# Two 16x16-head cross attentions: from folded context queries with turned probabilities to projected keys and values on 32-row and 32-column tiles

## The reference, cut to what matters

```python
qh = (q @ Wq + bq).reshape(B, LQ, HEADS, D_K).transpose(0, 2, 1, 3)      # LQ 64, HEADS 16, D_K 16
kh = (k @ Wk + bk).reshape(B, LKV, HEADS, D_K).transpose(0, 2, 1, 3)     # LKV 1601
vh = (v @ Wv + bv).reshape(B, LKV, HEADS, D_K).transpose(0, 2, 1, 3)
scores = jnp.einsum('bhqd,bhkd->bhqk', qh, kh) * scale                   # scale 1/4
attn = jax.nn.softmax(scores, axis=-1)
out = jnp.einsum('bhqk,bhkd->bhqd', attn, vh)
return concat @ Wo + bo
```

## Time and profile before

| what | value |
|---|---|
| three runs | 6370.2, 6377.44, 6382.16 us |
| the profiled execution, span from first to last instruction | 6363.3 us |
| its own time apart from the span | none is listed; the median lies 14.1 us above the span |
| TensorE busy, mean granted clock | 5521.9 us (87%), 0.901 |
| VectorE, ScalarE, GpSimd busy | 3835.9, 2546.1, 1134.8 us |

### The profile page before, as it was taken

How to read it: one execution, slowest core, us unless ns; L and a number is a source line. 1 busy time by engine, 2 the same in 40 slices (tenths; PEclk the granted TensorE clock), 3 DMA queues, 4 the chain that set the end, 5 groups by cost and what they waited for, 6 DMA issues and landing times. The chain is left out here.

```text
span 6363.3 us, 96853 instructions
## 1 busy us (share of the span) xinstructions
PE 5521.9 (87%) x33712; PEld 4579.4 (72%) x33712; DVE 3835.9 (60%) x7029; ACT 2546.1 (40%) x5011; POOL 1134.8 (18%) x545
## 2 busy tenths in 40 slices
PE   6789999976898999998655999885699899999877
PEld 4578888954797988886212888771499798889465
DVE  5367777725444767775797443457533677777453
ACT  1145555511444555553221333340244455555121
POOL 0022222100121001110363212234222111010200
PEclk8899999996899999999766999997799999999985
DMA  1010000001110000000111111123110100000020
GB/s 57 26 32 14 19 20 14 7 34 47 40 46 27 19 20 13 19 19 18 40 46 40 47 52 40 48 67 93 50 49 26 28 18 19 19 19 6 28 88 27
DMA packets 224813, 213.50 MB, mean 34 GB/s; under 512 B 54595, under 2 KB 201892, under 8 KB 216260
## 3 DMA queue, kind: packets, MB, share of 16 engines
q1 hardware_dynamic: 220356, 200.15, 10.3%
q10 hardware_dynamic: 4096, 8.40, 0.5%
HBM read 170.61 MB, written 2.23 MB: 27 GB/s over the span
## 5 line engine op out<-in xcount | busy, mean ns | idle before, releaser
L844 PE MATMUL PS<-context_turned,queries 128*128 128x512 f32 x4800 | 1127.3, 379 | 70.6 <-issue 54.2
L905 ACT CAST probs_turned<-PS 128x512 fp32r<-128x512 f32 x1600 | 726.6, 510 | 904.5 <-PE PS L856 904.5
L876 PE MATMUL PS<-probs_turned,context_part 128*128 128x256 f32 (+2 forms) x8112 | 1069.2, 286 | 8.1 <-DVE weighted L953 8.1
L919 DVE TENSOR_TENSOR probs_turned<-PS,probs_turned 128x512 fp32r<-128x512 f32 x1600 | 866.1, 583 | 299.8 <-ACT probs_turned L905 293.7
L844 PEld LDWEIGHTS PS<-context_turned,queries 128*128 128x128 f32 x4800 | 853.6, 194 | 235.7 <-issue 64.5
L876 PEld LDWEIGHTS PS<-probs_turned,context_part 128*128 128x128 f32 (+1 forms) x8112 | 996.0, 189 | 9.1 <-DVE probs_turned L919 9.1
L911 ACT ACTIVATE probs<-PS,minus_max 128x1024 f32<-128x1024 f32 (+1 forms) x800 | 747.6, 936 | 197.8 <-DVE minus_max L964 195.4
L959 DVE TENSOR_REDUCE row_max<-PS 128x1 f32<-128x1024 f32 (+1 forms) x800 | 757.1, 981 | 104.8 <-PE PS L844 104.1
L856 PE MATMUL PS<-ident,probs 128*128 128x128 f32 (+1 forms) x5200 | 734.5, 278 | 16.7 <-DVE probs_turned L919 13.1
L856 PEld LDWEIGHTS PS<-ident,probs 128*128 128x128 f32 (+1 forms) x5200 | 577.3, 140 | 62.9 <-issue 18.3
L1632 PE MATMUL PS<-input_part,part_up 128*128 128x512 f32 x2304 | 552.6, 392 | 18.5 <-DVEq L1713 8.6
(11 more groups left out here) (373 smaller groups left out, 6483.9 us busy)
## 6 DMA issues: line engine op xcount, KB each, us to landing
context_rows<-in_ctx SPq DMA_DIRECT2D x56, 768.0 KB
raw_up<-in_L_ffn_W SPq DMA_DIRECT2D x16, 1024.0 KB, 4.8
raw_down<-in_L_ffn_W SPq DMA_DIRECT2D x16, 1024.0 KB, 4.8
b_all<-bc_turned SPq DMA_DIRECT2D x16, 512.0 KB, 3.6
c_all<-bc_turned SPq DMA_DIRECT2D x16, 512.0 KB, 4.7
raw_up<-in_L_ffn_wg_w SPq DMA_DIRECT2D x8, 1024.0 KB, 4.8
raw_down<-in_L_ffn_w_w SPq DMA_DIRECT2D x8, 1024.0 KB, 4.8
raw_second<-in_L_ffn_w_w SPq DMA_DIRECT2D x8, 1024.0 KB, 6.9
```

The costliest lines, as they stand in the source:

```text
L844: last = nc.tensor.matmul(S[:, 512 * j:512 * j + cols], qs[a][:, v, p * P:(p + 1) * P], yT[b][:, v, 512 * j:512 * j + cols], start=(m == 0 ...
L876: last = nc.tensor.matmul(O_ps, yp[a][0:kk, u, k, :], probsT[b][0:kk, par, k, :], start=(k == 0 and m == 0), stop=(k == KT - 1 and m == 2))
L905: nc.scalar.copy(out, bank).then_inc(t_act.sem, 1)
L919: nc.vector.tensor_tensor(rest, bank, lead, ALU.subtract).then_inc(t_dve.sem, 1)
```

## The change

Both sublayers get an attention of their own, `head_attention`; `small_xattn` is rewritten around it. 16 dimensions of Wq are loaded per head instead of 32 (the DMA picks 16 of every 32 columns), so the queries need two chunks of 128 rows instead of four. `masked_queries` writes each chunk twice, with every other head zeroed: ScalarE writes the even heads and VectorE, after it, the odd ones, so that the 32 rows of two heads by 128 columns are one operand for both heads. Keys (turned, 256 x 1601) and values (1601 x 256, with a column of ones behind each head for the row sum) are made per batch with float32 matmuls. Scores are made twice in float32: as rows (128 queries x 512 keys), from which only the maximum is taken, and turned (128 keys x 128 queries, with the maximum subtracted by a matmul with ones into the same bank), from which ScalarE makes the exponentials that are the moving operand of the weighted sum as they are. No probability is transposed. Score matmuls use 32 rows of the array each, for four pairs of heads i = 0 to 3 into four banks; the weighted sum uses 128 rows and 17 columns at 32-column offsets, also four at a time, into one bank.

A batch is 7 units (`turns`) of two key tiles or one block of 512 keys, the last one short. A cycle t does the turned scores of unit t, values of unit t+10, the weighted sum of unit t-1, keys of unit t+12, row scores of unit t+8, and in L1 the context transposes of unit t+13 (four of the seven units); in L3 the context, stored turned to DRAM by L1, is loaded turned. There are 112 units and 13 + 3 further cycles around them. Two score fills per cycle share a ring of six banks; everything else (values, the turned maximum, the spread row sums, keys, context) shares one bank, `side`, and the weighted sum has the eighth. Every loop is written out, no hardware loop is left in these sublayers. Wo is loaded into four chunks of 128 rows of which half are zero, so `linear_rows` runs over 4 chunks instead of 2, and `turn_sums` goes.

```diff
@@ -1877,37 +1877,555 @@
 def l1_xattn(core):
-    small_xattn(core, "L1_xattn_", True)
+    small_xattn(core, "L1_xattn_", True, True)
...
-def small_xattn(core, pre, biased):
-
-    heads, d, pad = 16, 16, 32
-    X = core.X
+    small_xattn(core, "L3_xattn_", False, False)
+
+
+def small_xattn(core, pre, biased, first):
...
+        w = weights(core, own, pre, WkT=[P, 4, CDIM], Wv=[P, DIM])
+        w["Wq"] = core.sb(own, "wq", [P, DC, DIM])
+        loads = w.loads + [(w["Wq"][:, c, :].rearrange("p (h d) -> p h d", d=16),
+                            core.dram[pre + "Wq"][:, c, :].rearrange("p (h e) -> p h e", e=32)[:, :, 0:16], landed)
+                           for c in range(DC)]
...
-        sums = core.sb(own, "sums", [P, BATCH, heads // 2, d])
-        qT = core.sb(own, "qT", [P, heads * pad // P, TOKENS])
-        room = ContextRoom(core, own, 1, heads * pad // P, P // pad)
...
+        room = TurnedContext(core, own, first)
+        Q = core.sb(own, "queries", [P, DC, BATCH, 2 * SEQ])
+        oT = core.sb(own, "oT", [P, 4, TOKENS])
+        wo = core.sb(own, "wo_grouped", [P, 4, DIM])
+        made = HeadConstants(core, own, biased)
         with ExitStack() as front:
             U = core.sb(front, "u", [P, TILES, DIM])
             uT = core.sb(front, "uT", [P, DC, TOKENS])
-            normalize(core, X, U, loads=w.loads + room.loads, clear=room.q_tile, turned=(uT, None, None))
-            linear_turned(core, uT, w["Wq"], qT, w["bq"] if biased else None)
-        wv4 = w["Wv"][:].rearrange("c (a p d) -> c p a d", a=2, d=d)
-        context_attention(core, room, qT, head_queries(w["WkT"]), 4, heads * SEQ, False, None,
-                          lambda pair: wv4[:, pair], sums, heads // 2, 2, 2, 2, d ** -0.5, d)
-        oT = core.sb(own, "oT", [P, DC, TOKENS])
-        turn_sums(core, sums, heads // 2, d, oT, w["bv"])
-        linear_rows(core, oT, w["Wo"], X, w["bo"] if biased else None, X)
+            with nc.allow_non_contiguous_dma(reason="two bias rows of 256 numbers"):
+                normalize(core, X, U, loads=loads + room.loads, turned=(uT, None, None))
+            masked_queries(core, uT, w, Q, made, biased)
+        head_attention(core, room, Q, made, w["Wv"], biased, wo, core.dram[pre + "Wo"], oT, 0.25)
+        linear_rows(core, oT, wo, X, w["bo"] if biased else None, X)
...
+def masked_queries(core, src, w, Q, made, biased):
...
+            for f in range(fills):
+                m, half = f // HALVES, f % HALVES
+                for c in range(DC):
+                    last = nc.tensor.matmul(PS[:, f, :], w["Wq"][:, c, m * P:(m + 1) * P], src[:, c, half * 512:(half + 1) * 512],
+                                            start=(c == 0), stop=(c == DC - 1))
+                last.then_inc(ready.sem, 1)
...
+                nc.scalar.activation(out, bank, ACT.Identity, bias=made.bq[:, c, 0:1] if biased else 0.0,
+                                     scale=mask[:, 0:1]).then_inc(by_act.sem, 1)
...
+class TurnedContext:
...
+        self.y = [core.sb(own, "context_turned", [CDIM, KEYS]) for _ in range(2)]
+        self.landed = core.semaphores("context_landed", 2)
+        if first:
+            self.rows = [core.sb(own, "context_rows", [P, KT, CDIM]) for _ in range(2)]
...
+def head_attention(core, room, Q, made, wv, biased, wo, wo_rows, oT, scale):
...
+    s_lead, v_lead, k_lead, c_lead = 8, 10, 12, 13
+    ring, banks, side, out_bank = 3, 6, 6, 7
...
+    turn_at, spread_at = -1, 8
...
+    def st_fill(t):
+        return 4 * (min(t + s_lead, total) + t)
+
+    def s_fill(t):
+
+        return 4 * ((t + s_lead) + min(max(t + 1, 0), total))
+
+    def wait_fill(pe, fill):
+
+        if fill < banks:
+            return
+        old = fill - banks
+        for t in cycles:
+            if unit(t) is not None and st_fill(t) <= old < st_fill(t) + 4:
+                pe.wait_ge(exp_done.sem, exp_done.at(t * 4 + old - st_fill(t) + 1))
+            if unit(t + s_lead) is not None and s_fill(t) <= old < s_fill(t) + 4:
+                pe.wait_ge(max_done.sem, max_done.at((t + s_lead) * 4 + old - s_fill(t) + 1))
...
+        kT = core.sb(own, "keys_turned", [P, 2, DC, KEYS])
+        V = core.sb(own, "values", [P, 2, KT, heads, wide])
+        probs = core.sb(own, "probs_turned", [P, ring, groups, 2, DC, P])
+        part = core.sb(own, "block_max", [P, 2, DC, groups, 4])
+        M = core.sb(own, "row_max", [P, groups, 32])
+        shift = core.sb(own, "minus_max", [P, 2, DC, P], F32R)
+        ones = core.sb(own, "ones_wide", [P, P], F32R)
+        O = core.sb(own, "weighted", [P, 2, 4 * SEQ])
...
+                        sp.wait_ge(side_dve.sem, side_dve.at(dve_no["context", b * turns + context_fills - 1] + 1))
+                        sp.dma_start(core.dram["ctx_turned"][b], room.y[b % 2][:]).then_inc(stored[b % 2].sem, 16)
...
+                def wait_side(fill):
+                    n = fill_no[fill]
+                    if n:
+                        by, count = taken_by[n - 1]
+                        pe.wait_ge(by.sem, by.at(count + 1))
...
+                    for k in range(4 * j, min(4 * j + 4, KT)):
+                        kk = keys_of[k]
+                        last = nc.tensor.transpose(PS[:, side, (k - 4 * j) * P:(k - 4 * j) * P + kk], room.rows[b % 2][0:kk, k, :],
+                                                   core.ident[0:kk, 0:kk])
+                    last.then_inc(side_ready.sem, 1)
...
+                    for n, c in enumerate(chunks):
+                        last = nc.tensor.matmul(PS[:, side, n * cols:(n + 1) * cols], wk[:, c * P:(c + 1) * P],
+                                                room.y[b % 2][:, lo:lo + cols], start=True, stop=True)
+                    last.then_inc(side_ready.sem, 1)
...
+                    for n, kt in enumerate(tiles_of(j)):
+                        kk = keys_of[kt]
+                        last = nc.tensor.matmul(PS[0:kk, side, n * DIM:(n + 1) * DIM], room.y[b % 2][:, kt * P:kt * P + kk], wv[:],
+                                                start=True, stop=True)
+                    last.then_inc(side_ready.sem, 1)
...
+                    for i in range(groups):
+                        wait_fill(pe, s_fill(t) + i)
+                    for n, c in enumerate(chunks):
+                        for i in range(groups):
+                            rows = slice(32 * i, 32 * i + 32)
+                            last = nc.tensor.matmul(PS[:, (s_fill(t) + i) % banks, n * cols:(n + 1) * cols], Q[rows, c, b, :],
+                                                    kT[rows, b % 2, c, lo:lo + cols], start=True, stop=True)
+                    last.then_inc(s_ready.sem, 1)
...
+                    for i in range(groups):
+                        wait_fill(pe, st_fill(t) + i)
+                    many = len(tiles_of(j))
+                    for i in range(groups):
+                        rows = slice(32 * i, 32 * i + 32)
+                        nc.tensor.matmul(PS[:, (st_fill(t) + i) % banks, 0:many * 2 * P].rearrange("p (k s) -> p k s", k=many), ones[rows, :],
+                                         shift[rows, b % 2].rearrange("p c s -> p (c s)").unsqueeze(1).broadcast_to([32, many, 2 * P]),
+                                         start=True, stop=False, skip_group_check=True)
+                    for n, kt in enumerate(tiles_of(j)):
+                        kk = keys_of[kt]
+                        for c in range(DC):
+                            at = (n * DC + c) * P
+                            for i in range(groups):
+                                rows = slice(32 * i, 32 * i + 32)
+                                last = nc.tensor.matmul(PS[0:kk, (st_fill(t) + i) % banks, at:at + P],
+                                                        kT[rows, b % 2, c, kt * P:kt * P + kk], Q[rows, c, b, :],
+                                                        start=False, stop=True, skip_group_check=True)
+                    last.then_inc(st_ready.sem, 1)
...
+                    for n, kt in enumerate(tiles_of(j)):
+                        kk = keys_of[kt]
+                        for c in range(DC):
+                            for a in range(2):
+                                g = 2 * c + a
+                                for i in range(groups):
+                                    last = nc.tensor.matmul(PS[32 * i:32 * i + wide, out_bank, g * SEQ:(g + 1) * SEQ],
+                                                            V[0:kk, b % 2, kt, 8 * a + 4 * c + i, :],
+                                                            probs[0:kk, t % ring, i, n, c, a * SEQ:(a + 1) * SEQ],
+                                                            start=(kt == 0 and g == 0), stop=(kt == KT - 1), skip_group_check=True)
+                    last.then_inc(av_done.sem, 1)
...
+                for t in cycles:
+                    if unit(t) is not None:
+                        scores_turned(t)
```

(46 more changed lines are left out.)

310 lines of the change are left out of this document (305 added, 5 removed).

## The result

Five runs of the changed kernel have a median of 6321.36 us (6317.11 to 6333.05), five of the kernel before 6377.44 us (6349.16 to 6389.2). The ratio is 0.9924, with an interval of 0.9906 to 0.9943: 56 us less, where 263 were forecast. The direction was right, the size was not, and 6321 lies just outside the range, which ended at 6310.

What follows compares the result with a forecast made beforehand. TensorE was taken to bound the kernel, busy for 87% of 6363.3 us. Attention blocks -154 and -116 us, ends +7, total -263, gave a span of 6100 and a median of 6114 us; range for 8 in 10: 5900 to 6310.

Steps and rivals of the forecast that it cites:

- the prices of the records: TensorE in both attention blocks: float32 records cost 0.43 us for 512 columns, 0.22 for 256, 0.11 for 128.
- full overlap of the tiles: Scores and weighted sum: four float32 tiles run in about the time of one, 0.055 us a round of 64 columns.
- the changes of shape: Each attention cycle: four changes of tile shape at 0.2 us each, 28 a batch, 5.6 us.
- TensorE waits for the maxima once a cycle: Before the turned scores: 1.5 us in six cycles, 0.7 in the short one, 9.7 us a batch.
- B: Turned scores, row scores, weighted sum: tiles overlap by about three quarters, 30% more, +182 us, 6296 in all; chance 0.18.
- D: Weighted sum: column tiles reading the same 128 rows take turns, 22.8 instead of 5.7 us, +547, 6661; chance 0.06.
- Rival A: Both attention blocks: loads slip under the drain, so the 5.6 us of shape changes vanish, -179 us, 5935; chance 0.15.
- a batch at full clock, L3 and L1: Attention blocks: work, shape changes and waits sum to 47.7 us a batch in L3, 50.3 in L1.
- filling and emptying: Pipeline's 13 cycles of filling and 3 of emptying: +10 us in each block, bounds 0 and 40.
- fronts and ends: Around both attention blocks: front at zero (bounds -5 and +15), end +3.6 us for more Wo records less `turn_sums`.
- twice a batch a fill of the shared bank follows directly on another: Turned maximum after values, keys after spread sums: TensorE waits 0.9 us each, 1.8 us a batch.
- Rival C: Both attention blocks: TensorE's idle time drops the clock, at 1.2 GHz +1160 us, 7270 in all; chance 0.09.

Runs made afterwards that it cites:

- the copy: Against the changed kernel, the spread row sums are copied out of the shared bank first and inverted from SBUF: 6243.07 us, ratio 0.9799 to the kernel before.
- the busy wait: Against the changed kernel, ten records of an unread identity product run on TensorE while it waits for the division: 6264.43 us, ratio 0.9824 to the kernel before.
- the kernel of all together: Changed kernel plus copy before division, values first, busy filling, ScalarE's context copy and a later wait for GpSimd's constants: 5986.9 us, 0.9389 to the kernel before.
- one moved call: Against the changed kernel, values are made before the turned scores in cycles without context transposes just before: 6111.03 us, ratio 0.9604 to the kernel before.

## Why the prediction was wrong in size

**Right: the prices of the records, full overlap of the tiles, the changes of shape, and that TensorE waits for the maxima once a cycle.** Rivals B and D fall: 64 weighted records of 17 columns and 128 rows take 1.02 us from start to start, change of shape included, where 16 x 0.055 + 0.2 = 1.08 was priced and D had four times the records' part. The 8 row-score records on four row tiles take 1.14 us and the 2 key records on the full array 1.13, so four tiles cost what one costs, to 0.01 us. The Trainium skill, in "TensorE: Matmul & The Clock Gate", Measured speedup vs the span model, gives 3.07 for four row tiles; the measurement here decides, and it says 4. Rival A falls too: priced at 0.86 to 0.88 us, the bursts are 1.02 to 1.06 us apart, so that 0.14 to 0.20 us for the change of shape are in every one. The Trainium skill's rule in "TensorEngine Tiling (Array Packing)", Key Properties, that a change of mode drains the engine, agrees with it.

**Wrong: three terms (the waits of a batch, no loss of clock in the steady cycles, the filling), and a rival that was taken as all or nothing.** Between the two profiled executions -263 was forecast and 6326.3 - 6363.3 = -37 measured, 226 us apart. They go to these steps:

| step of the prediction | forecast | measured | part of the 226 us |
|---|---|---|---|
| a batch at full clock, L3 and L1 | 47.7, 50.3 | 50.6, 52.0 | 16 x 2.9 + 16 x 1.7 = 74 |
| the clock in the steady cycles | no loss | 54.3 - 50.6, 53.5 - 52.0 | 16 x 3.7 + 16 x 1.5 = 83 |
| filling and emptying | +10 each | block less 16 middle batches: 26 in L3, 46 in L1 | 52 |
| fronts and ends | +3.6 each | +5.7 in L3, +11.1 in L1 | 10 |
| the unchanged code, mostly from L1's end to L3's start | 0 | 1969.9 after, 1963.6 before | 7 |

The first row holds the step "twice a batch a fill of the shared bank follows directly on another, 0.9 us each". It took every evacuation of that bank for a copy of 0.69 us. One of them is a reciprocal of 256 columns, and that takes 1.76 us:

```profile
L2383 DVE RECIPROCAL row_scale<-PS 128x256 f32<-128x256 f32 x16 | 28.1, 1758 | 34.6 <-PE PS L2284 34.6
```

This could have been read before. The kernel before has reciprocals of other widths (VectorE by shape, the kernel before):

```profile
L552 DVE RECIPROCAL row_sum<-row_sum 128x16 f32<-128x16 f32 x24 | 6.1, 253 | 0.8
L1403 DVE RECIPROCAL variance<-variance 128x64 f32<-128x64 f32 x1 | 0.6, 553 | 2.1 <-PEq L1414 2.1
```

From 16 to 64 columns 300 ns are added, 6.25 ns a column; 553 + 192 x 6.25 = 1753 ns for 256. The term would have been 0.17 + 0.07 + 1.75 = 2.0 instead of 0.9, and 1.94 was measured: one microsecond a batch at full clock, 33 us in all.

The other 40 us of that row are cycles priced too low, by 0.3 us each in L3 and 0.1 in L1. In L3 this is the wait for the maxima. The forecast counted its 1.5 us from the end of streaming, that is from 0.86 us after the first row-score record started; so counted it is 5441.03 - 5438.38 - 0.86 = 1.79 us. The 1.50 us that the profile lists start at the record's end, 1.14 us after its start, and that both numbers are 1.5 is luck. The record runs 0.28 us past the streaming and not 0.17, VectorE starts 0.07 us later and needs 2 x 0.62 us for two maxima, and then another 0.2 us pass before TensorE starts, for which the forecast had no term. VectorE in the undisturbed cycle:

```profile
5439.59 2.48 DVE L2350 TENSOR_REDUCE block_max<-PS 128x1 f32<-128x512 f32 x4 [2.48 <-PE PS L2231]
```

The second row is the larger error. Rival C asked whether the clock stays up, priced its loss for whole blocks only, and set it aside with "here no wait is forecast longer than 1.5 us". That held for the waits of 1.50 us, which repeat in nearly every cycle at full rate. It didn't hold for one of 1.94 us, and that one came from the mis-priced division: the copy and the busy wait both show it, the copy by taking 37 us of waiting and giving 78 us, the identity products by giving 57 us with the wait left in. Around the division a batch lost 3.7 us more in L3 and 1.5 in L1. The copy gave back some 2.0 and 1.2 of these; that the rest is the division's too, through the maxima that it delays, is argued and not shown.

The third row: "each stage waits for its predecessor through the one shared bank" was written down, and then +10 us taken. In the filling there is nothing but such hand-overs, one of 0.8 us behind every 2 us of work, and the clock was 0.58 and 0.63 through all of it. L1, with three stages instead of two, paid most and lies beyond the bound of 40. Keeping TensorE busy there gave back 26 us.

Of the fronts, 4 us in each sublayer are a wait for GpSimd's constants that the prediction had put on VectorE. The median of before lies 14.1 us above its profiled span; the changed kernel's profiled run took 6328.03 us, 1.7 above its own span. So those 14 us were mostly the difference between runs. The last row of the table can be of that kind too: in the profiled runs of the experiments the time from L1's last matmul of `head_attention` to L3's first, 2019.8 us in the changed kernel, went from 2015.6 to 2026.8 us with the code between them unchanged (the kernel of all together left out, whose L3 begins its matmuls 4 us earlier).

What stays open: why some batches lose the clock after the 1.94 us wait and others don't (of the thirteen middle batches of the changed kernel 4 kept it in L1 and none in L3; in L3 with ten identity records 5 kept it, at equal waits by the trace), and the rare waits for "issue" of up to 3.46 us. The prediction had put such waits down to the hardware loop; here one stands in written-out code.

## What to carry to other kernels

Where a pipeline leaves TensorE waiting every cycle, look first for work in the same cycle that needs neither the bank nor the operand that is waited for, and put it there: one moved call was worth more than everything that the change itself brought. Price each evacuation of a shared bank by its own operation and width, from the nearest rows in the trace, since a division isn't a copy, and let a copy free the bank. And price a wait twice, once by its length and once by the clock after it: where it is longer than those that the stream has been seen to stand, shorten it or give the engine something to do in it.

## What the runs showed of the hardware

- A reciprocal on VectorE costs 6.3 to 6.9 ns a column (1758 ns for 256), from PSUM or from SBUF alike (1.76 and 1.75 us); a copy of the same 256 columns takes 0.42 us.
- A granted clock can fall for some 10 us and come back. Behind a wait of 1.94 us in a stream that is otherwise busy three quarters of the time, 32 turned scores took 1.94 us instead of 1.09, and 10 us later the rate was full again. Waits of 1.50 us in the same stream left the rate as it was, except right behind that of 1.94 and in the first cycle behind the filling. Length alone doesn't decide: with the copy first, the records behind a wait of 1.75 us were slow in 14 of 14 places of L3 behind the spread sums, but not behind one of 1.75 us elsewhere.
- Work that nobody reads can make a kernel faster: ten records of 128 columns a batch gave 57 us, and six after each step of the filling 38 us.
- Four column tiles of 17 columns that read the same 128 rows overlap fully in float32: 64 records of 64 columns in 1.09 us, where 16 records one after the other, at 0.055 us each, would take 0.88 and the change of shape 0.14 to 0.20.
